# Cross attention over 32 sequences: a later hand-over of each result, a constant carried by a contraction row, transposed maxima in a bank of their own

## The reference, cut to what the change touches

Only the first half of the second layer matters here: cross attention with 16 heads of 8 channels, keys and values from a context of 96 channels.

## Time and profile before

| | us |
|---|---|
| three timed runs, median (lowest to highest) | 881.33 (880.14 to 882.28) |
| the profiled execution, its own time | 877.17 |
| its span in the profile | 875.3 |
| of the span: attention1, from its first to its last instruction | 264.3 to 486.1 |
| busy in the whole span: PE, DVE, ACT, POOL | 723.7, 616.0, 428.0, 216.2 |

### The profile page before, as it was taken

How to read it: one execution, slowest core, us unless ns; L and a number is a source line. 1 busy time by engine, 2 the same in 40 slices (tenths; PEclk the granted TensorE clock), 3 DMA queues, 4 the chain that set the end, 5 groups by cost and what they waited for, 6 DMA issues and landing times. The chain is left out here.

```text
span 875.3 us, 25351 instructions
## 1 busy us (share of the span) xinstructions
PE 723.7 (83%) x9696; PEld 524.0 (60%) x9696; DVE 616.0 (70%) x1801; ACT 428.0 (49%) x777; POOL 216.2 (25%) x326
## 2 busy tenths in 40 slices
PE   3457988889796898889889477788768999999997
PEld 2334554556464665566567246566556888888886
DVE  7568887878776777777776478788555666666653
ACT  3022333223243787667766266566623555554553
POOL 3343223332418033321100453243011110111100
PEclk9957999899796999989999589999987999999999
DMA  4000000041035212222110000000000000000000
GB/s 102 9 21 13 23 21 21 20 90 27 12 83 123 73 51 58 60 77 79 50 42 14 6 2 4 4 4 5 4 4 1 14 12 0 12 12 12 12 13 13
DMA packets 33078, 26.36 MB, mean 30 GB/s; under 512 B 9740, under 2 KB 29912, under 8 KB 32984
## 3 DMA queue, kind: packets, MB, share of 16 engines
q1 hardware_dynamic: 29944, 24.07, 10.5%
q10 hardware_dynamic: 3040, 0.98, 0.5%
HBM read 13.51 MB, written 7.34 MB: 24 GB/s over the span
## 5 line engine op out<-in xcount | busy, mean ns | idle before, releaser
L1948 PEld LDWEIGHTS bank<-w2r,hme 128*128 128x128 f32 x1024 | 132.3, 192 | 15.8 <-ACT hme L1893 1.4
L1948 PE MATMUL bank<-w2r,hme 128*128 128x128 f32 x1024 | 135.6, 276 | 0.0
L1893 ACT ACTIVATE hme<-bank,b 128x512 f32<-128x512 f32 x128 | 86.5, 687 | 97.5 <-PE bank L104 97.4
L1917 DVE SCALAR_TENSOR_TENSOR Xq<-bank,wgte,Xq 128x128 f32 (+1 forms) x256 | 72.1, 343 | 52.4 <-PE bank L1948 39.6
L1004 ACT ACTIVATE P<-bank,shift 128x512 f32<-128x512 f32 x128 | 87.7, 691 | 12.9 <-PE bank L1146 10.9
L1083 DVE TENSOR_REDUCE mx<-bank 128x4 f32<-128x512 f32 x128 | 87.6, 685 | 4.9 <-PE bank L1125 4.5
L1076 DVE TENSOR_SCALAR P<-P 128x512 f32<-128x512 f32 x128 | 58.6, 458 | 43.6 <-ACT P L1004 43.6
L520 ACT ACTIVATE w2r<-bank 128x512 f32<-128x512 f32 x40 | 23.9, 597 | 115.4 <-PE bank L833 84.3
L1165 PE MATMUL bank<-P,V 128*32 128x128 f32 x1024 | 47.9, 287 | 11.7 <-DVE P L1076 11.5
L102 PE MATMUL bank<-xTe,w 128*128 (+1 forms) x128 | 49.2, 385 | 5.4 <-PEq L1312 5.4
L1723 POOL TENSOR_SCALAR rs<-mv 128x4 f32<-128x4 f32 x8 | 1.6, 194 | 201.8 <-DVE mv L1785 201.8
(11 more groups left out here) (382 smaller groups left out, 1798.2 us busy)
## 6 DMA issues: line engine op xcount, KB each, us to landing
cross_q<-qh SPq DMA_DIRECT2D x24, 128.0 KB
Q<-cross_q SPq DMA_DIRECT2D x8, 384.0 KB, 3.5
X<-in_x SPq DMA_DIRECT2D x8, 256.0 KB, 2.8
Xq<-X SPq DMA_DIRECT2D x32, 64.0 KB
cross_k<-kh SPq DMA_DIRECT2D x16, 128.0 KB
Yq<-Y SPq DMA_DIRECT2D x32, 64.0 KB
out_x<-Xq SPq DMA_DIRECT2D x32, 64.0 KB, 1.7
cload<-in_ctx SPq DMA_DIRECT2D x8, 192.0 KB, 2.5
```

Of the source, the lines that this page charges most:

```text
L1893: act.activation(hm[:, p % HR], UP[p % RING][:], ACT.Gelu_apprx_tanh, bias=b1[:, p:p + 1]).then_inc(s["gelu"], 1)
L1917: last = dve.scalar_tensor_tensor(x, Y[f % 2][:, 128 * i:128 * i + 128], w, x, ALU.mult, ALU.add)
L1948: last = pe.matmul(Y[f % 2][:, cols], hm[:, p % HR, cols], w2r[:, p], start=(p % 2 == 0 and i == 0), stop=(p % 2 == 1), skip_group_check=True)
```

```diff
+def minus_columns(pool, minus, ident, sem):
+
+    pool.tensor_scalar(minus[KEY_ROWS:128, :], ident[KEY_ROWS:128, KEY_ROWS + 4:KEY_ROWS + 5].broadcast_to([32, NH // 4]),
+                       -TOP_GAP, 0.0, ALU.mult, ALU.add).then_inc(sem, 1)
+    pool.wait_ge(sem, 1)
+    pool.tensor_tensor(minus[KEY_ROWS:128, :], minus[KEY_ROWS:128, :], ident[KEY_ROWS:128, KEY_ROWS:KEY_ROWS + NH // 4],
+                       ALU.subtract).then_inc(sem, 1)
+    pool.wait_ge(sem, 2)
...
-    RING = 4
+    RING = 6
...
-        SB, TB = [S0, S1], [T0, T1, T2]
-        M = O[0:32, 2 * S:4 * S].bitcast(F16)
+        SB, TB = [S0, S1], [T0, T1]
+        M = T2[0:32, 0:2 * S].bitcast(F16)
...
-                after(act, s["o_psum"], u - 3)
-                act.activation(P[j][:], TB[u % 3][:], ACT.Exp, bias=c["shift"][:], scale=SCALE).then_inc(s["p_exp"], 1)
+                after(act, s["o_psum"], u - RING + 1)
+                act.activation(P[u % RING][:], TB[u % 2][:], ACT.Exp, scale=SCALE).then_inc(s["p_exp"], 1)
...
-            dve.memset(m16[:], 0.0)
+            dve.memset(m16[:], 0.0).then_inc(s["m_clear"], 1)
+            dve.wait_ge(s["m_clear"], 1)
+            dve.memset(m16[:].rearrange("p (h r) -> p h r", h=4)[:, :, U:U + 1], 1.0)
...
             def step(b):
                 maxima(b + 1, 0)
+                normalise(b - 3)
+                clip(b - 1, 1)
+                maxima(b + 1, 1)
+                clip(b - 1, 2)
+                maxima(b + 1, 2)
                 clip(b - 1, 3)
-                maxima(b + 1, 1)
-                clip(b, 0)
                 prepare(b // 4, b % 4)
-                maxima(b + 1, 2)
-                clip(b, 1)
                 maxima(b + 1, 3)
...
-                clip(b, 2)
...
+                clip(b, 0)
...
-                after(pe, s["p_exp"], U * b + j - 2)
+                after(pe, s["p_exp"], U * b + j - 1)
...
-            for b in range(-1, B + 2):
+            for b in range(-1, B + 3):
```

More of the change, by code:

```diff
@@ L1002, in exp @@
                 act.wait_ge(s["t_psum"], u + 1)
[L1003 to L1004 removed]
+                after(act, s["o_psum"], u - RING + 1)
+                act.activation(P[u % RING][:], TB[u % 2][:], ACT.Exp, scale=SCALE).then_inc(s["p_exp"], 1)
             def step(b):
                 n, i = b // 4, b % 4
+                if has(b - 2):
+                    act.wait_ge(s["o_psum"], U * (b - 1))
+                    after(act, s["f_psum"], b - 2)
+                    act.activation(OE[:], O[:], ACT.Copy).then_inc(s["oT_sb"], 1)
+                if has(b - 1):
+                    exp(b - 1, 2)
                 if has(b):
@@ L1012, in step @@
                 if has(b - 1):
-                    exp(b - 1, U - 1)
+                    exp(b - 1, 3)
+                if has(b - 3):
+                    act.wait_ge(s["a_psum"], b - 2)
+                    after(act, s["y_psum"], b - 3)
+                    act.activation(OT[:], F[:, 0:S], ACT.Copy).then_inc(s["a_sb"], 1)
+                prepare(n, i)
                 if has(b):
                     exp(b, 0)
[L1016 to L1024, removed]
+                if has(b - 3):
+                    act.wait_ge(s["y_psum"], b - 2)
+                    after(act, keep["yq_in"][(b - 3) % 4], 16 * ((b - 3) // 4))
+                    act.activation(Y[:, (b - 3) % 4, :], F[:, S:2 * S], ACT.Copy).then_inc(s["y_ready"], 1)
                 if has(b):
                     exp(b, 1)
[L1027 to L1032, removed]
                 low(n + 2, i)
@@ L1197, in step @@
                     score(b1, 0)
-                if has(b):
-                    turn_max(b)
                 if has(b - 1):
-                    score_t(b - 1, 3)
+                    score_t(b - 1, 2)
                 prepare(b // 4, b % 4)
@@ L1208, in step @@
                 if has(b):
-                    score_t(b, 0)
-                if has(b - 2):
-                    pe.wait_ge(s["o_norm"], b - 1)
+                    turn_max(b)
+                if has(b - 1):
+                    score_t(b - 1, 3)
+                if has(b - 3):
+                    pe.wait_ge(s["o_norm"], b - 2)
                     pe.transpose(F[:, 0:S], On[:], ident[:]).then_inc(s["a_psum"], 1)
                 if has(b - 1):
-                    values(b - 1, 2)
-                    values(b - 1, 3)
+                    values(b - 1, 0)
+                    values(b - 1, 1)
                 if has(b1):
@@ L1229, in step @@
                 if has(b):
[L1230 to L1234, removed]
+                    score_t(b, 1)
+                if has(b - 2):
+                    pe.wait_ge(s["oT_sb"], b - 1)
+                    after(pe, s["y_ready"], b - 2)
+                    if b == 2:
                         pe.wait_ge(s["small_const"], 2)
@@ L1238, in step @@
                     last.then_inc(s["f_psum"], 1)
[L1239 to L1242, removed]
+                if has(b - 1):
+                    values(b - 1, 2)
+                    values(b - 1, 3)
+            for b in range(-1, B + 3):
                 step(b)
```

44 lines of the change are left out of this document (28 added, 16 removed).

## The result

The changed kernel takes 853.67 us (median of four runs, 850.61 to 857.17) where the kernel before takes 880.74: a ratio of 0.969, with a 95% interval of 0.965 to 0.9735. It is clearly faster.

A forecast was written before the change was run, and what follows sets the result against it. Bound by a ring of waits, not an engine's work. Steps 2 to 30 -18.1, beginning -1.5, end +2.0 make -17.6: 877.2 profiled becomes 859.6, plus 4.2 to the median gives 863.7 us, range 857.5 to 873.

The forecast's parts named there:

- The ring of waits: Cross attention's plain step: linked waits between engines, without slack, set its 5.73 us; PE alone would need 4.5.
- The terms: Six parts of the new plain step, from PE's first score to the next, summing to 5.24 us against 5.73.
- The chunks: Four steps of cross attention together: 23.25 us against 26.21, 2.95 less each, -11.8 over chunks 1 to 4.
- The step with i = 1: A chunk's step with projection: 5.8 us, then 6.0 because DVE's low half and statistics spill over by some 0.25.
- The clock: Chunks 3 and 4 carry 1.2 and 2.0 us of lowered TensorE clock; only half counted as gained, -1.6.
- Rival 3: Waits before On-turn and F-turn let the clock fall, 1.8 us a step; twelve more such steps give 885; chance 0.04.
- Beginning and end: Cross attention's start gains 1.5 us at clips held beside POOL's filling of K; a pipeline one step deeper costs 2.0.
- The memsets: Chunk 5: POOL's memset was assumed to go on holding a clip there as before; chunk 5 gains 2.0 us in all.
- costed at nothing: Side effects priced at zero, among them two small POOL instructions of `minus_columns` in layer0, under 0.5 us without cover.
- rival 4: POOL's normalisation of x holds clips, one or two holds of 0.86 us per chunk, 5 to 8.6: 871; chance 0.03.
- from the profiled execution to the median: Whole kernel: 859.6 us profiled plus 4.2, the old median's excess over its profiled execution, gives 863.7.
- The sum for the stage: Cross attention: -18.1 for steps 2 to 30, -1.5 at the beginning, +2.0 at the end, in all -17.6 us.

The follow-up runs named there:

- e1: The kernel before plus the two small POOL instructions of `minus_columns`, result unused, ahead of layer0's first `negative_rows`: 0.9947 of the kernel before, 4.7 us faster.
- e3: The kernel before, old order and banks, with only the new constant (exponential without bias), `minus_columns` early: 0.9954 of the kernel before, 4.0 us faster.
- e8: The kernel before with layer0's `negative_rows` behind xnB, Kd's memsets cut into sixteen, second K set's `negative_rows` in 32 pieces: 0.9952 of the kernel before, 4.2 us faster.
- e6: The changed kernel with Kd's two memsets cut into sixteen of 256 columns, no waits between them: 0.972 of the kernel before.
- e2: The changed kernel with `minus_columns` moved to the beginning of layer0, so `negative_rows` starts as early as before: 0.9764 of the kernel before.
- e5: The changed kernel with POOL's `negative_rows` of layer0 waiting until DVE has written xnB: 0.9719 of the kernel before.
- e4: The changed kernel with the old bias and old `negative_rows` back, keeping new order, banks and ring of six: 0.9814 of the kernel before, 16.3 us faster.
- e10: The changed kernel with Kd's memsets cut into sixteen, POOL waiting for the end of each before issuing the next: 0.9671 of the kernel before.
- e7: The changed kernel with layer0's `negative_rows` behind xnB, Kd's memsets cut into sixteen, second K set's `negative_rows` in 32 pieces: 0.9722 of the kernel before.

## Why the prediction was right or wrong

**What bounds the kernel: right.** The ring of waits was the step. When the clip and OE left it, the plain step went to what the sum said, 5.21 for 5.24, with no engine made faster by more than the 0.09 of an exponential. The terms came out one by one: 1.67, 1.06, 0.43, 0.49, 0.42 and 1.13 in step 26, for 1.73, 1.0, 0.44, 0.52, 0.41 and 1.14.

**The chunks: right, in part by luck.** 23.05 for 23.25. Step 8's kind lost the most, 7.39 to 5.46 from first score to first score, because low half and statistics no longer stand before clips that PE needs. The step with i = 1 is 0.16 longer than forecast and the other three are 0.10 to 0.14 shorter, which cancels in part.

**The clock: half counted, wholly gained.** Chunks 3 and 4 lost 3.3 us to it before, and I counted 1.6. All four profiles of the old order (before, e1, e3, e8) have steps with i = 1 over 7 us, at a clock of 0.65 to 0.84, in chunks 2 to 4; none of the ten with the new order has one there. That is 1.6 more. Rival 3 did not come. In the old order these steps stand behind one with i = 0 in which PE sits idle for 1.8 to 1.9 us, and not every such step is followed by a lower clock (4 and 8 of the kernel before are not). With the change PE sits idle for 0.25 in step 12 and 0.47 in step 13. That the shorter waits keep the clock up fits all fourteen profiles, but no run tested it alone. PE's busy share of a chunk does not settle it: chunks 2 and 3 have 1.00 at 22.05 busy of 23.05 with the change, and chunk 1 of the kernel before had 1.00 at 22.72 of 26.21.

**Beginning and end: right within 1 in this pair of profiles.** From the stage's first instruction to the third Q copy 2.3 us were won (1.5 forecast), from the last Q copy to the last Y 2.3 lost (2.0 forecast). But that beginning, 22.3 in the kernel before, took 24.3 in e1 and e3, which have the old order too, so the gain there may be up to 4.4. The last Q copy came 25.1 earlier in the span (18 to 20 forecast): 20.0 of these lie in the stage and 5.1 in layer0.

**The memsets: undersized.** "The hold of a clip there by POOL's memset stays, I assume" failed. It grew from 2.30 to 3.83, PE's wait for it from 1.82 to 2.76, and the clock, 1.00 before in that step, fell to 0.67, so chunk 5 took 27.35 for 24.8 forecast. In chunk 1 another row of memsets held a clip for 1.97, 0.9 us of a chunk. Together 3.4 us against the gain, which about cancel the better clock and beginning, so that the stage came out at 17.7 for 17.6. That so close a number came out is luck.

**The step that failed: "costed at nothing".** The forecast had "two more small POOL instructions of `minus_columns` stand in layer0, in place of a memset; with no cover, under 0.5." They were worth -4.7 us (e1), ten times the bound and of the other sign, because four DVE instructions beside POOL's next ones went from 7.93 us to 2.71. I priced them as work and asked only what covers them. I did not ask what POOL's next instructions do to another engine, and when. The row had shown a hold of that kind, and the place in layer0 was in the same trace.

**POOL beside DVE: one case taken for all.** From the earlier trace rows I took it that POOL's normalisation holds no clip, and that was right as far as it went: rival 4, with its holds of 0.86, did not come, and the clips beside a normalisation took 0.42 to 0.60 in the kernel before and 0.41 to 0.52 in the changed one. But I stopped there and did not ask it of the rest of POOL's work, though a clip took 1.73 beside `negative_rows`. In the earlier trace rows it is the normalisation that is longer beside a clip; of its four, the first has the clip of the earlier trace rows beside it and the second has none:

```profile
334.65 0.93 POOL L196 TENSOR_SCALAR xn<-X,mv,rs 128x128 f32<-128x128 f32 x1
```
```profile
335.57 0.79 POOL L196 TENSOR_SCALAR xn<-X,mv,rs 128x128 f32<-128x128 f32 x1
```

What the traces show differs from one kind of POOL's work to the next. Beside the memsets of Kd a clip of 0.42 took 2.30 before and 3.83 with the change; beside `negative_rows` an instruction of xnB took 2.04 for its 0.34; beside the normalisation of x a clip took 0.42. To start first did not help: the first instruction of xnB before started 0.05 ahead of POOL's, at 61.91, and was the one that took 2.04. And in e6 one clip, 4.38 long, ended only after all sixteen memsets of the row.

**The second step that failed: from the profiled execution to the median.** I forecast 859.6 for the profiled execution, and it took 857.17. To 859.6 I added the 4.2 us by which the three timed runs lay above the profiled one. In the three later sets the median of the kernel before was 875.8 to 878.7, about that of its profiled execution, so the 4.2 belong to that set of runs and not to the kernel. The 10.0 us between 863.7 and 853.67 are, in numbers, the 4.2 that I added, 2.4 by which the profiled execution was faster than forecast, and 3.5 by which the median of the changed kernel lies below its own profiled execution.

**The sum for the stage: short by about 3.** Single profiled executions scatter by as much as these differences, and the ratios of many runs say more. By them (e2) the cross attention gained 20.7 us (18.5 to 22.8), where the sum had 17.6, and layer0 about 4.7, where the forecast had nothing. So the 17.7 of one pair of profiles agrees with the sum in part by luck. Up to 2 of the missing 3 us can be the beginning of the stage (24.3 in e1 and e3 for 22.3); no run settles it.

**Not settled.** Why the clips take 0.41 to 0.60 beside the normalisation of x and up to 4.38 beside the memsets, and why a clip got in between pieces of `negative_rows` and not between the memsets of e6. The records of those memsets overlap (0.31 long, 0.25 apart), those of the pieces do not (0.40 long, 0.47 apart or more); whether that is the reason was not tested. Theory A of e1 and e5 has its name from a port, and no run shows one: they show only how long the instructions of both engines took. Nor was it tried to free the three holds at the beginning without lengthening POOL's work.

## What to carry to other kernels

Follow the ring of a step, link by link, before counting any engine's work: which result is consumed in the step that makes it? Handing the results over a step later took the plain step from 5.73 to 5.30 here with the order alone (e4), and cost 2.3 us at the end. Then look at every place where GpSimd fills memory beside VectorE, in all of the program and not only where the change lies: a shift of 0.56 us in its queue was worth 4.7 us in one direction (e1) and some 4.5 in the other (e2). Where it must fill by memsets, try them cut short with a wait for each, if nothing that is needed stands behind them: that was worth 3.6 us here (e10), and the cut alone brought nothing (e6, 0.972 for 0.971).

## What the runs showed of the hardware that was not expected

- Four VectorE instructions, started 0.05 us before four GpSimd ones of 1.90, took 7.93 us together; with GpSimd 0.56 us later, 2.71; with GpSimd behind them, 1.12.
- A VectorE clip of 0.42 us took 3.83 behind two GpSimd memsets of 1.80 and 4.38 behind sixteen of 0.31 without waits between them; with a wait between each two, 0.41 to 0.58. Among GpSimd tensor_scalars of 256 columns without waits (e7) it took 0.41 to 0.59.
- Clips beside GpSimd's normalisations of x took 0.42 to 0.60 before and 0.41 to 0.52 with the change. The normalisation beside the clip of the earlier trace rows took 0.93, and the next, without a clip, 0.79.
- `negative_rows` cut into 32 pieces of 256 columns took 16.1 us where four of 2048 took 8.0: 0.40 each with nothing beside them, but 0.50 from one to the next in the mean.
